# Moving work inside the first and the last batches of a fused attention and FFN kernel

## The reference, cut to what matters

```
xn  = rms_norm(x) * g_norm * (1 + scale) + shift      # scale, shift = cond @ W_emb + b_emb
q, k, v = xn @ W_qkv, 16 heads of 32; q, k = rms_norm(q) * g_q, rms_norm(k) * g_k
o   = softmax(q @ k.T / sqrt(32)) @ v
y   = o + o @ W_out
h   = gelu(layer_norm(y) @ ternary(w_fc).T)            # 512 -> 2048
out = x + layer_norm(h) @ ternary(w_proj).T            # 2048 -> 512
```

## Time and profile before

| | |
|---|---|
| median of 3 runs | 1168.1 us (1166.49 to 1168.19) |
| time of the profiled execution | 1165.45 us |
| its span | 1163.6 us |
| busy: PE, DVE, ACT, POOL | 1075.8, 895.6, 814.5, 543.1 us |
| mean granted TensorE clock | 0.968 |
| iteration 0, about | 48.8 to 122 |
| heads of iteration 15, about | 1075.6 to 1110 |
| iterations 16 and 17 | 1110 to 1163.6 |

### The profile page before, as it was taken

The page is one execution under the profiler, slowest core; times in us unless marked ns, Lnnn a source line. Parts: engine busy times, 40 slices in busy tenths (PEclk is TensorE's granted clock), DMA queues, the critical chain, the costliest instruction groups (busy, mean ns, idle before and its releaser), DMA issues.

```text
span 1163.6 us, 26244 instructions
## 1 busy us (share of the span) xinstructions
PE 1075.8 (92%) x9484; PEld 675.8 (58%) x9484; DVE 895.6 (77%) x1616; ACT 814.5 (70%) x1372; POOL 543.1 (47%) x365
## 2 busy tenths in 40 slices
PE   5646899999999999999999999999999999999797
PEld 1324565666666565666666565666666566666463
DVE  4668768888788888878787888878787888877544
ACT  4866575867768586877768586876868586775752
POOL 1522173643718173553718174463808264462425
PEclk8868899999999999999999999999999999999889
DMA  9810303112130313112031212112131212002101
GB/s 341 302 28 1 92 20 74 56 36 57 38 90 36 72 54 72 54 25 66 36 90 36 72 54 54 55 33 75 36 90 36 72 54 45 29 25 50 38 1 55
DMA packets 75501, 74.20 MB, mean 64 GB/s; under 512 B 6592, under 2 KB 56000, under 8 KB 74944
## 3 DMA queue, kind: packets, MB, share of 16 engines
q1 hardware_dynamic: 75456, 73.59, 21.7%
HBM read 39.89 MB, written 8.39 MB: 41 GB/s over the span
## 4 chain that ended last, share of the span: by engine, by line
PE 74%; DVE 11%; ACT 9%; issue 3%; DMA 1%; SPq 0%; DVEq 0%; ACTq 0%; POOL 0%
PE F L625 10%; PE F L627 10%; PE F L782 5%; PE F L783 5%; PE QA L593 3%; PE QA L594 3%; PE QA L595 3%; PE QB L593 3%; PE QB L594 3%; PE QB L595 3%; DVE rowmax L1088 2%; PE T L813 2%; PE SA L681 2%; DVE xn_lo L1075 2%; PE SB L681 2%
## 5 line engine op out<-in xcount | busy, mean ns | idle before, releaser
L552 POOL TENSOR_TENSOR rqk<-ssq,half 128x16 f32<-128x16 f32 x64 | 186.8, 2920 | 93.6 <-DVE ssq L1241 93.4
L782 PE MATMUL F<-yT_hi,fc_t 128*128 128x256 f16 x1024 | 227.7, 274 | 0.0
L783 PE MATMUL F<-yT_lo,fc_t 128*128 128x256 f16 x1024 | 227.3, 273 | 0.0
L625 PE MATMUL F<-proj_t,hs 128*128 128x512 f16 x512 | 196.6, 384 | 3.8 <-DVE hs L1206 3.8
L627 PE MATMUL F<-proj_t,hs 128*128 128x512 f16 x512 | 196.1, 383 | 0.0
L1206 DVE SCALAR_TENSOR_TENSOR hs<-hg,g_inv,hs 128x512 f16<-128x512 f32 x128 | 142.3, 1112 | 46.4 <-ACT hs L922 44.5
L520 POOL TENSOR_TENSOR acc<-acc,hg 128x512 f32<-128x512 f32 x96 | 148.0, 1542 | 8.6
L527 POOL TENSOR_TENSOR acc<-acc,hq 128x512 f32<-128x512 f32 x96 | 123.1, 1282 | 18.4 <-ACT hq L978 8.1
L917 ACT ACTIVATE hg<-F,g_fc 128x512 f32<-128x512 f32 x128 | 87.5, 684 | 52.9 <-PE F L783 51.3
L514 POOL TENSOR_TENSOR rs<-var,half 128x1 f32<-128x1 f32 x32 | 17.6, 550 | 226.4 <-DVE var L1099 226.4
L1220 DVE TENSOR_TENSOR p_lo<-SA,p_hi 128x512 f16<-128x512 f32 x128 | 88.0, 687 | 42.0 <-ACT p_hi L938 41.8
(11 more groups left out here) (192 smaller groups left out, 2753.0 us busy)
## 6 DMA issues: line engine op xcount, KB each, us to landing
stk<-qkT SPq DMA_DIRECT2D x128, 128.0 KB, 2.5
xtok<-in_x SPq DMA_DIRECT2D x16, 512.0 KB, 3.6
xT_sb<-in_xT SPq DMA_DIRECT2D x16, 512.0 KB, 3.4
stk<-qkT SPq DMA_DIRECT2D x128, 64.0 KB, 2.1
xres<-in_x SPq DMA_DIRECT2D x16, 512.0 KB, 3.6
out<-xres SPq DMA_DIRECT2D x16, 512.0 KB, 2.8
stk<-in_w_emb SPq DMA_DIRECT2D x4, 512.0 KB, 5.5
fc_t<-in_w_qkv SPq DMA_DIRECT2D x2, 1024.0 KB, 12.1
```

The lines of the kernel that those rows point to most:

```text
L552: pool.tensor_tensor(rqk[:, n % 2, :], ssq[:, n % 2, :], half[:, :], ALU.pow).then_inc(rqk_r, 1)
L625: pe.matmul(FB[t][:, :], hs[:, 0, k // 2, col:col + P], proj_t[:, k, :], start=(k == 0), stop=False)
L782: pe.matmul(dst, w, yT_hi[:, k, :], start=(k == 0), stop=False)
L783: mm = pe.matmul(dst, w, yT_lo[:, k, :], start=False, stop=(k == KT - 1))
```

## The change: what it does

1. In iteration 0 the DVE's mean square moves from unit 2 to unit 7, behind the last maxima and the first ternary pass. On ACT the two squares of the input move ahead of the magnitudes, the roundings and the split of `w_out`.
2. In the heads of iteration 0 the ternary passes (DVE) and the roundings (ACT) move to the end of their head, behind the other work of that head.
3. In the heads of iteration 15 a list of its own, `LAST_FILLER`, gives PE one unit of PROJ1 at heads 0, 1, 2, 3, 5, 7, 9 and 11, in place of two at 2 and 3 and one at 4, 7, 10 and 11. PROJ0[0:2] stays at head 13, behind the stats turn of head 12.
4. In every batch, `second(b, t, e)` waits for low part e + 1 instead of all eight at e = 0. For t = 1 it waits for seven GELUs instead of eight.
5. In iteration 16 ACT makes the squares 0, 1 and 2 in units 2, 4 and 6, and the squares 3 to 7 behind unit 7, where it made one in each unit. POOL adds all hidden values first and then all squares, where it took them in turns.
6. The output of batch 15 is written by two DMAs of 256 KB, one for each half, each as soon as its half is done.

```diff
+LAST_FILLER = {0: PROJ1[0:1], 1: PROJ1[1:2], 2: PROJ1[2:3], 3: PROJ1[3:4], 5: PROJ1[4:5], 7: PROJ1[5:6],
+               9: PROJ1[6:7], 11: PROJ1[7:8], 13: PROJ0[0:2]}
...
+def msx_unit(i):
+
+    return UNITS - 1 if isinstance(i, int) and i == 0 else MSX_UNIT
...
                 if late is not None:
-                    sp.wait_ge(out_r, nth(late, TT, TT))
-                    sp.dma_start(out_t[late], xres[:, :, :]).then_inc(st_out, 16)
+                    if isinstance(late, int) and late == B - 1:
+                        sp.wait_ge(out_r, nth(late, TT, tile_no(1)))
+                        sp.dma_start(out_t[late][:, 1:TT, :], xres[:, 1:TT, :]).then_inc(st_out, 16)
+                        sp.wait_ge(out_r, nth(late, TT, tile_no(0)))
+                        sp.dma_start(out_t[late][:, 0:1, :], xres[:, 0:1, :]).then_inc(st_out, 16)
+                    else:
+                        sp.wait_ge(out_r, nth(late, TT, TT))
+                        sp.dma_start(out_t[late], xres[:, :, :]).then_inc(st_out, 16)
...
                     if att is None:
                         for n in range(1, UNITS):
                             add_h(n)
+                        for n in range(1, UNITS):
                             add_q(n)
...
                 def second(b, t, e):
                     if e == 0:
-                        pe.wait_ge(gelu_r, nth(b, UNITS, UNITS))
-                        pe.wait_ge(hlo_r, nth(b, UNITS, UNITS))
+                        pe.wait_ge(gelu_r, nth(b, UNITS, UNITS - t))
+                    pe.wait_ge(hlo_r, nth(b, UNITS, e + 1))
...
-                if isinstance(i, int) and i == 0:
-                    magnitudes(1, PROJ_ABS_ORDER[2])
-                    magnitudes(1, PROJ_ABS_ORDER[3])
-                    for k in range(4):
-                        rounded(0, k)
-                    act.wait_ge(wo_i, KT)
-                    act.activation(wo_hi ...)
                 (layer norm, yT_hi, then the two squares of the input)
+                if isinstance(i, int) and i == 0:
+                    (the same block)
...
-                        if att is None:
-                            square_hidden(ffn, n)
-                        elif n in HSQ_UNIT:
+                        if n in HSQ_UNIT:
                             square_hidden(ffn, HSQ_UNIT[n])
+                if ffn is not None and att is None:
+                    for n in range(len(HSQ_UNIT), UNITS):
+                        square_hidden(ffn, n)
...
-                    if n == MSX_UNIT and pre is not None and not first(pre):
+                    if n == msx_unit(i) and pre is not None and not first(pre):
                         mean_square(pre)
...
-                    (DVE: ternary(0, FC_AT[h]), ternary(1, PROJ_AT[h]) directly behind p_lo of head h)
+                    (the same behind heads_lo, ssq, qkn, the piece's low part and the rms work of head h)
-                    (ACT: rounded(1, PROJ_ROUND_AT[h]) directly behind p_hi of head h)
+                    (the same behind sq, the piece's high part and heads_hi of head h)
```

More of the change, by code:

```diff
@@ L123, in filler @@
 def filler(i, h):
-    return FIRST_FILLER.get(h, []) if isinstance(i, int) and i < 0 else FILLER[h]
+    if isinstance(i, int) and i < 0:
+        return FIRST_FILLER.get(h, [])
+    if isinstance(i, int) and i == B - 1:
+        return LAST_FILLER.get(h, [])
+    return FILLER[h]
 def square_at(b):
@@ L487, in _ @@
                 iteration(i)
-            sp.wait_ge(st_out, nth(B - 1, 16, 16))
+            sp.wait_ge(st_out, nth(B - 1, 16, 32))
         @block.gpsimd
@@ L877, in iteration @@
                     qkv_weights((2,))
-                if isinstance(i, int) and i == 0:
-                    magnitudes(1, PROJ_ABS_ORDER[2])
-                    magnitudes(1, PROJ_ABS_ORDER[3])
-                    for k in range(4):
-                        rounded(0, k)
-                    act.wait_ge(wo_i, KT)
-                    act.activation(wo_hi[:, :, :].rearrange("p k n -> p (k n)"), wo_raw, ACT.Identity,
-                                   scale=WO_SCALE).then_inc(wo_h, 1)
                 if ffn is not None:
@@ L906, in iteration @@
                                        ).then_inc(ssx_r, 1)
+                if isinstance(i, int) and i == 0:
+                    magnitudes(1, PROJ_ABS_ORDER[2])
+                    magnitudes(1, PROJ_ABS_ORDER[3])
+                    for k in range(4):
+                        rounded(0, k)
+                    act.wait_ge(wo_i, KT)
+                    act.activation(wo_hi[:, :, :].rearrange("p k n -> p (k n)"), wo_raw, ACT.Identity,
+                                   scale=WO_SCALE).then_inc(wo_h, 1)
                 if ffn is not None:
@@ L944, in iteration @@
                         magnitudes(1, PROJ_ABS_AT[h])
-                    if isinstance(i, int) and i == 0 and h in PROJ_ROUND_AT:
-                        rounded(1, PROJ_ROUND_AT[h])
                     if qkv is not None and h in square_at(qkv):
@@ L967, in iteration @@
                         heads_hi(i, att, n)
+                    if isinstance(i, int) and i == 0 and h in PROJ_ROUND_AT:
+                        rounded(1, PROJ_ROUND_AT[h])
                 if qkv is not None:
@@ L1224, in iteration @@
                         magnitude(0)
-                    if isinstance(i, int) and i == 0 and h in FC_AT:
-                        ternary(0, FC_AT[h])
-                    if isinstance(i, int) and i == 0 and h in PROJ_AT:
-                        ternary(1, PROJ_AT[h])
                     if isinstance(i, int) and i == 1 and h == COLSUM_AT:
@@ L1286, in iteration @@
                         dve.tensor_scalar(c2[:, :], rs2[:, :], g_both[:, 0:1], None, ALU.mult).then_inc(c_r, 1)
+                    if isinstance(i, int) and i == 0 and h in FC_AT:
+                        ternary(0, FC_AT[h])
+                    if isinstance(i, int) and i == 0 and h in PROJ_AT:
+                        ternary(1, PROJ_AT[h])
                     if h == OUT1_AT and ffn is not None:
```

## The result

The changed kernel takes 1155.57 us (median of 4 runs, 1154.22 to 1156.19), the kernel before beside it 1168.14 us (1166.49 to 1168.29). The ratio is 0.990, 95% interval 0.9889 to 0.9914: 11.6 us less, between 10.0 and 13.0. The forecast was 1161.3 with a range from 1157.2. The direction was right, and the gain came out larger than the range allowed, by 1.6 us.

A forecast was written before the change was run, and what follows sets the result against it. PE was taken to bound the steady stretches, a chain through all engines iterations 0 and 15 to 17; -3.5 - 3.0 - 1.7 + 0 + 0.6 + 1.65 - 0.8 = -6.75 from 1168.1 gave 1161.3 us, range 1157.2 to 1165.5.

The forecast's parts named there:

- The size of edit 2: Heads of iteration 0: passes moved last shorten PE's waits; walked through as 3.8 us, taken as -3.0, bounds 0 and -5.8.
- The size of edit 3: Iteration 15: spread units fill PE idle and let ACT start head 3 sooner; -1.7 us, bounds -0.5 and -3.0.
- The base: Whole kernel: the median of the runs, 1168.1 us, lies 2.65 us above the profiled execution; the terms were subtracted from it.
- Edit 1: Start of iteration 0: without DVE's wait for the squares the first `p_lo` comes sooner; -3.5 us.
- Edit 5: Iteration 16: POOL's additions bring the fold later, +0.6 us, and PROJ0 runs at half clock behind the idle, +1.65 us.
- Edit 4's step: Every batch: the added waits on PE are satisfied long before in iterations 1 to 15 and cost 0.
- Edit 1's covers: Iteration 0: the mean square's delay is covered, and nothing in ACT's block waits for the input, loaded in iteration -1.
- 1 (heads give nothing): Heads of iteration 0: every pass moved pushes the next `p_lo` by what it freed; 1164.3 us, chance 0.21.
- 5 (nothing): Whole kernel: iteration 0's gain is given back and the end loses what iteration 15 wins; 1167.9 us, chance 0.07.
- 3 (the end is not POOL's): Iteration 16: additions overlap, PE goes straight on from PROJ1 and gains 3.8 us; 1155.3 us, chance 0.04.
- 4: Every batch: the new waits cost PE time, at 0.05 us each the kernel takes 1172.6 us; chance 0.05.
- Rival 2: Iterations 0 and 15: all gains come, -5.8 for the moved passes and -3.0 for the units; 1157.2 us, chance 0.15.

The follow-up runs named there:

- b_ternary: The kernel before with only the ternary passes and roundings of iteration 0 moved to the end of their head: 1162.07 us, ratio 0.9961.
- n_ternary_dve: The kernel before with only DVE's ternary passes moved to the end of their head, ACT's roundings left in place: 1161.13 us, ratio 0.9953.
- o_rounds_back: i_statsmid with ACT's four roundings put back directly behind the high part of their head: 1146.99 us, ratio 0.9826.
- k_warm15: The kernel before plus 18 matmuls with overwritten results behind the scores of heads 0 and 1 of iteration 15: 1162.20 us, ratio 0.9960.
- c_units15: The kernel before with only iteration 15's PROJ1 units spread out, and own-low-part waits for batch 14 only: 1163.33 us, ratio 0.9978.
- d_end: The kernel before with own-low-part waits in every batch and iteration 16's squares and POOL additions reordered, output in one DMA: 1171.14 us, ratio 1.0036.
- i_statsmid: The changed kernel with DVE adding iteration 16's squares and four units of PROJ0 before the stats turn, four behind it: 1146.32 us, ratio 0.9826.
- l_warmend: The changed kernel plus 28 matmuls with overwritten results between PROJ1 and the stats turn of iteration 16: 1152.50 us, ratio 0.9878.

## Why the prediction was right and where it was wrong

**Right in kind, too small in size.** Every edit did what its step said, at the place it said. "Alone" is the delta of the table above:

| step | forecast | profile | alone |
|---|---|---|---|
| edits 1 and 2, iteration 0 | -6.5 | -9.12 | -4.7 and -4.6 |
| edit 3, iteration 15 and the step behind it | -1.7 | -2.43 and -1.10 | -2.6 (-4.0 to -1.2) |
| edit 4, steady batches | 0 | +0.06 in 792 us | with edit 5: +4.2 |
| edit 5, GELUs to the fold | +0.6 | +1.20 | |
| edit 5, clock on PROJ0 | +1.65 | +2.17 | |
| edit 6 | -0.8 | -0.82 | not tried alone |

The forecast, 1161.35 before rounding, was 5.8 us too long. Half of that is in the terms (-6.75 forecast, -9.6 in the profiles), half in the base. Three steps failed.

**The size of edit 2**: "the walk gives 3.8 for edit 2 ... I take 3.0". Behind the first `p_lo`, where edit 2 acts, 5.45 us came in after and 5.62 in b_ternary. The walk itself was short: it had the last `p_lo` 7.3 us sooner, and it came 8.18 us sooner (3.67 + 4.51); it had the iteration's end 7 to 8 us sooner, I booked 6.5, and it came 9.12 us sooner, of which 0.94 is the clock behind the last `p_lo`. And the discount was wrong. My reason for it, "PE stays gapped" at a clock of 0.79, pointed the other way: with the gaps closed the clock of the heads rose to 0.84 and that of the whole iteration by 0.07, and PE's busy time shrank by 1.93 us. n_ternary_dve and o_rounds_back show that the gain is from DVE's passes.

**The size of edit 3**: "I take -1.7 us". It was 3.53 us in the two stages, 2.43 and 1.10. The 1.7 came from ACT's wait of 1.96 us, and that wait shrank by 1.61, as it said. What the step counted no gain for is the clock: 1.28 of the 2.43 and all of the 1.10 us, as PE's busy times show, so 2.4 of the 3.53. k_warm15 confirms it: it raises the clock alone, and gains 4.7 us with the old order of units.

**The base**: "The median of the runs is 1168.1, 2.65 above the profiled one". The forecast carried these 2.65 us over to the changed kernel as a constant. But the profiled execution of after is 0.3 us above its median, so the distance was not one: 2.95 us. A likely part of it is the length of iteration 15, which varies with the clock. Before was profiled in a short one (123.40; others of that order 123.99 to 126.07), and the new order varies less (120.83 to 120.97, and 121.71 in c_units15). So edit 3 gains more against the median than against that one profile. How much of the 2.95 us, and of the missing 3 us between 8.5 (the parts) and 11.6 (the whole), this explains stays open: only one execution of each kernel was profiled.

**Edit 1** was right to 0.2 us up to the first `p_lo` (3.67 for 3.5). Alone it gave another 1.1, nearly all of it clock behind the last `p_lo`, which the step did not have.

**Edit 5** was named with its sign, against what the order suggests, and d_end confirms it. The fold came another 0.6 us later than forecast. 0.4 of that is an error of addition: 1141.4 + 2 x 1.7 + 5 x 1.22 is 1150.9 and not 1150.5, which makes the term +1.0. The other 0.2 is what three errors leave. The last GELU came 0.3 us sooner than forecast, and POOL's last addition of a hidden value took 1.27 us and not 1.71. But the squares then took 10.42 us on POOL (1128.49 to 1138.91) and not 9.5: 1.72 for the first and 8.56 for the other six, whose starts are 1.41 us apart from the second on, where I took 1.7 twice and then 1.22. The 1.22 was read where hidden values and squares took turns. Each addition waits for the one before it into the same sum; with turns another addition stood between the two, and now none does. That this is why their starts are 0.19 us further apart is argued from the order and was not tried. The clock's cost was 2.17 for 1.65, since the stats turn is slow too (1.87 us; 0.95 in i_statsmid). l_warmend measures that term by itself: 2.27.

**Edit 6** came out as forecast, -0.82 us for -0.8. The formula of the Trainium skill that the prediction sets beside it (DMA: Bandwidth & Descriptors, Anatomy of one DMA) stands there for transfers that GpSimd issues, and this one is issued by SP; it gave 0.6.

**Edit 4's** step holds: 224 more waits, 0.06 us. **Edit 1's covers** held in after but not always: "nothing in this block waits for it" was wrong, as o_rounds_back's 1.03 us shows.

**The rivals.** 1 (heads give nothing) and 5 (nothing) fall by b_ternary, 3 (the end is not POOL's) by the 8.26 us of idle behind POOL's additions, 4 by iterations 2 to 13. Rival 3's time, 1155.3, is the nearest to the measured 1155.6, for the wrong reason. Rival 2 (all of it comes) is nearest to what happened: edit 2 at -5.5 of -5.8 and the stages of edit 3 at -3.5, past its bound of -3.0; with the end's loss larger than forecast. Its sum of -10.9 is 1.3 us more than the profiles show, and its time of 1157.2 is still too long, by the base.

## What to carry to other kernels

Work that must be done anyway is not free to stand anywhere: put a long pass behind everything in its stage that another engine waits for, if its own result is not needed before. Where a stretch alternates between idle and work, count what closing a gap does to the clock of the matmuls behind it, and do not discount a walked-through gain for slow clock without asking if the gain changes the clock. Take the base of a forecast and the profile that its terms are read from as two things: one profiled execution can lie 2.7 us off its median. At the end of a kernel look at what each engine does in the last wait: here two edits that looked like savings cost 4.2 us, and the wait they made was worth 9 us once it was filled with work that was still to do.

## What the runs showed of the hardware

- **More matmuls, less time.** 18 matmuls that compute nothing made the kernel 4.7 us faster (k_warm15), 28 made it 3.1 us faster (l_warmend), by keeping the granted clock at 1.00 in stretches where it had fallen to 0.50.
- **A satisfied wait on PE shows no price**: 14 more in each batch, 0.06 us in twelve iterations of 65.96.
- **DVE beside POOL.** The residual of 128x512 takes 0.74 us when POOL is idle (i_statsmid) and 1.75 us while POOL adds, in after:

```profile
1128.49 1.72 POOL L544 TENSOR_TENSOR acc<-hq 128x512 f32<-128x512 f32 x1
...
1128.99 1.75 DVE L1162 SCALAR_TENSOR_TENSOR xres<-res,c,xres 128x512 f32<-128x512 f32 x1
```

  The Trainium skill (SBUF — State Buffer, Who interferes with whom) has them exclude each other for the whole of an instruction. By that, as an estimate, the residual would wait from 1128.99 for POOL's end at 1130.21 and, with its 0.75 us, end at 1130.96; it ended at 1130.74. The trace agrees within 0.2 us.
- **An addition of 128x512 floats** takes 0.69 us on DVE and 1.26 on POOL when the other is idle, and up to 1.72 on POOL beside DVE. Additions into the same sum start 0.80 us apart on DVE (six in 4.67, i_statsmid) and 1.41 apart on POOL (in after). The Trainium skill (GPSIMD Engine Reference, Elementwise — side-by-side cycle accounting) has a ratio of 1.96 for an addition of 2048 elements; here it is 1.8 for 512 (1.26 to 0.69).
- **The output in halves**: 256 KB landed in 2.0 us and 512 KB in 2.8, so that the last transfer is 0.8 us shorter.
